# Attention without transposed probabilities: a second score product with keys on partitions, sums by paired GpSimd adds, three projection banks

## What is computed

```python
Q = (layernorm(x) @ Wq + bq)        # 16 x 224 x 512, split into 16 heads
K = (ctx @ Wk + bk)                 # 16 x 750 x 512
V = (ctx @ Wv + bv)
scores = Q K^T / sqrt(32) * gate    # gate: per key, from a second context tensor
out = softmax(scores) V
x = x + tanh(g_xattn) * (out @ Wo + bo)
x = x + tanh(g_ffn) * ffn(layernorm(x))   # shared and routed experts, top 2 of 16
```

## Time and profile before

| | |
|---|---|
| median of 3 executions | 2176.14 us |
| the profiled execution, span of its core | 2176.1 us |
| first batch's loop, from the first V product on | 69.0 to 162.3 us |
| batches 1 to 14, each | 94.7 us |
| last batch and the end of the attention | 1487.6 to 1581 us |
| experts phase | about 595 us |
| busy in the span | PE 94%, PEld 77%, DVE 58%, ACT 44%, POOL 27% |
| DMA | 307 MB, mean 141 GB/s |

### The profile page before, as it was taken

The page is one execution under the profiler, slowest core; times in us unless marked ns, Lnnn a source line. Parts: engine busy times, 40 slices in busy tenths (PEclk is TensorE's granted clock), DMA queues, the critical chain, the costliest instruction groups (busy, mean ns, idle before and its releaser), DMA issues. The chain is left out here.

```text
span 2176.1 us, 43249 instructions
## 1 busy us (share of the span) xinstructions
PE 2043.5 (94%) x13700; PEld 1677.6 (77%) x13701; DVE 1272.2 (58%) x2344; ACT 953.6 (44%) x1983; POOL 582.8 (27%) x682
## 2 busy tenths in 40 slices
PE   4999999999999999999999999999716999999999
PEld 4788888988888898888879888887514666678887
DVE  4557565665756566575666657565584333345555
ACT  0456565645656464565646556465411222210000
POOL 4222231322213132221313212130034333323331
PEclk9999999999999999999999999999956999999999
DMA  5645555554555555455555545554273444435543
GB/s 176 174 115 158 134 136 153 130 144 116 157 135 136 151 131 145 121 150 138 136 154 129 144 126 143 140 137 110 54 302 95 145 144 145 145 107 168 168 139 115
DMA packets 176438, 307.17 MB, mean 141 GB/s; under 512 B 29344, under 2 KB 86688, under 8 KB 176048
## 3 DMA queue, kind: packets, MB, share of 16 engines
q1 hardware_dynamic: 163008, 265.30, 44.4%
q0 software_dynamic: 10880, 33.56, 5.6%
q10 hardware_dynamic: 2512, 7.82, 0.9%
HBM read 145.03 MB, written 63.24 MB: 96 GB/s over the span
## 5 line engine op out<-in xcount | busy, mean ns | idle before, releaser
L631 DVE TENSOR_REDUCE neg_max<-score 112x1 f32<-112x750 f32 x512 | 455.9, 932 | 46.5 <-PE score L843 42.4
L463 ACT ACTIVATE probs<-score,neg_max 112x750 f32<-112x750 f32 x512 | 448.1, 883 | 74.1 <-DVE neg_max L631 72.7
L866 PE MATMUL flip<-ident,probs 112*125 112x112 f32 x3072 | 420.6, 274 | 9.3 <-ACT probs_t L471 8.2
L471 ACT ACTIVATE probs_t<-flip 125x448 f32<-125x448 f32 x512 | 276.6, 543 | 328.4 <-PE flip L866 328.0
L866 PEld LDWEIGHTS flip<-ident,probs 112*125 112x125 f32 x3072 | 387.4, 188 | 41.6 <-ACT probs_t L471 15.7
L361 POOL TENSOR_TENSOR k_lo<-fresh,k_hi 128x376 fp32r<-128x376 f32 (+1 forms) x128 | 118.2, 923 | 448.3 <-ACT k_hi L491 448.3
L843 PE MATMUL score<-k_stack,q_stack 128*112 128x512 f32 (+1 forms) x1024 | 232.7, 348 | 3.2 <-ACT probs L463 3.2
L815 PE MATMUL proj<-ctx_hi,wk_hi 128*128 128x376 f32 (+1 forms) x512 | 183.7, 359 | 8.3 <-POOL ctx_lo L361 6.2
L639 DVE TENSOR_SCALAR probs_t<-flip 125x448 f32<-125x448 f32 x256 | 158.1, 617 | 45.8 <-PE flip L866 45.6
L815 PE MATMUL proj<-ctx_lo,wk_hi 128*128 128x376 f32 (+1 forms) x512 | 172.0, 336 | 0.0
L815 PE MATMUL proj<-ctx_hi,wk_lo 128*128 128x376 f32 (+1 forms) x512 | 171.9, 336 | 0.0
(11 more groups left out here) (189 smaller groups left out, 3175.9 us busy)
## 6 DMA issues: line engine op xcount, KB each, us to landing
k_stack<-k_hi SPq DMA_DIRECT2D x512, 93.8 KB, 2.2
k_stack<-k_lo SPq DMA_DIRECT2D x512, 93.8 KB, 2.2
q_stack<-q_parts SPq DMA_DIRECT2D x128, 224.0 KB, 3.6
ctx_raw<-in_ctx_t SPq DMA_DIRECT2D x64, 375.0 KB, 5.3
y_slots<-y_sb SPq DMA_DIRECT2D x72, 256.0 KB, 3.1
x_in<-in_x SPq DMA_DIRECT2D x16, 448.0 KB, 5.5
q_parts<-q_hi SPq DMA_DIRECT2D x64, 112.0 KB
q_parts<-q_lo SPq DMA_DIRECT2D x64, 112.0 KB
```

The lines of the kernel that those rows point to most:

```text
L463: act.activation(probs[0:QW, h % 2, t, :], score[t][0:QW, 0:S], ACT.Exp, bias=neg_max[:, h % 2, t:t + 1], accum_out=row_sum[:, t, h:h + 1] ...
L471: act.activation(probs_t[0:KW, h % HC, 2 * p:2 * p + 2, :].rearrange("k a q -> k (a q)"), flip[(3 * h + p) % 2][0:KW, 0:2 * L], ACT.Relu). ...
L631: nc.vector.tensor_reduce(neg_max[:, h % 2, t:t + 1], score[t][0:QW, 0:S], axis=AX.X, op=ALU.max, negate=True).then_inc(maxed[t], 1)
L866: ins = nc.tensor.transpose(flip[g % 2][0:KW, k * L + t * QW:k * L + (t + 1) * QW], probs[0:QW, h % 2, t, kt * KW:(kt + 1) * KW], ident[0: ...
```

## The change

The transposes of the probabilities go, and with them `probs`, `flip_probs`, `copy_flipped`, `reciprocals` and `spread_reciprocals`.

- A second score product, `score_columns`, has keys on partitions: `k_stack` is now the stationary side (98 rows x 125 keys) and `q_stack` the moving side (224 queries). For each head there are six of them, two to a tick; a group of four heads has 12 ticks, which are worked through in three phases of four ticks (one tick per head). ACT takes the exponential of a tick from PSUM straight into `probs_t` (`exponential`), 125 x 448, without a bias.
- The maximum is brought in by the product itself. The first score product (`score_rows`) stays and serves the maximum alone, in a single buffer of two banks, six heads ahead of the attended one. `split_shift` splits the maxima of a group in two parts, `turn_shift` transposes them on PE, `copy_shift` copies them out, and `place_shift`, a DMA in ACT's list, puts them into two further rows of `q_stack`, against rows of ones in `k_stack`.
- The row sums are made from the transposed tiles. POOL adds each phase's tiles, two heads at a time, into `acc` (`add_first`, `add_pair`: 10 adds of 125 x 448 per group), and `sum_up` multiplies `acc` with a matrix of ones, which sums over partitions and spreads over 32 rows at once. `normalize_output` on DVE takes the reciprocal of 128 x 224 sums.
- `attend` is cut into three calls per group, one per phase.
- The projection has three PSUM banks (`bank_of`) with semaphores of their own in place of one; `project_out` uses them too, and its eight products, the projections and the transposes are dealt out in small pieces between the ticks.
- The stack has 96 rows (three parts): per group 12 DMAs into `k_stack` and 2 into `q_stack` in place of 16 and 2, for all 16 heads (before: 8). `k_hi`, `k_lo`, `q_hi`, `q_lo` hold two groups (before: four).
- Work changes engines: the high part of the context, the scaling of the normalization, and the copies of transposes go from DVE to ACT; two of four context remainders and the query remainders go from POOL to DVE. `store_cols` goes from ACT's to SP's queue.
- Before the loop: K before Q, V items 0 to 3 in place of item 0, and scores of heads 0 to 5 in place of head 0.

The core of the diff:

```diff
+LOWEST = -3.4028234e38
...
+BODY = ("V4", "V5", "O0", "SH1", "O1", "XT0", "XT1", "K0a", "Q0", "K0b", "SH2", "Q1", "K1a",
+        "K1b", "K2a", "K2b", "K3a", "SH3", "K3b", "YT0", "YT1", "LG", "V0", "V1", "SH0", "V2", "V3")
+OF_LAST = ("O0", "O1", "YT0", "YT1", "LG")
+SETUP = ("XT0", "XT1", "K0a", "Q0", "K0b", "Q1", "K1a", "K1b", "K2a", "K2b", "K3a", "K3b", "V0", "V1", "V2", "V3", "SH0")
...
+BEFORE = len(SETUP) + len(FIRST) - ITEMS
...
-        probs = sb("probs", [P, 2, QT, S])
-        probs_t = sb("probs_t", [P, HC, KT, L])
+        probs_t = sb("probs_t", [P, 2, HC, 2 * L])
+        acc = sb("acc", [P, HC, L])
...
-        score = [ps(f"score{t}", [P, 1024]) for t in range(QT)]
-        flip = [ps(f"flip{i}", [P, 512]) for i in range(2)]
-        proj = ps("proj", [P, 512])
...
+        score = ps("score", [P, 1024])
+        st = [ps(f"st{i}", [P, 512]) for i in range(2)]
+        proj = [ps(f"proj{i}", [P, 512]) for i in range(BANKS)]
         pv = ps("pv", [P, 512])
...
-                    for row in range(4):
-                        k_sb = k_hi if row < 2 else k_lo
-                        sp.dma_start(k_stack[row * DH:(row + 1) * DH, ring * HC + j, :].bitcast(F32),
-                                     k_sb[j * DH:(j + 1) * DH, c, :].bitcast(F32)).then_inc(k_stacked[ring], 16)
...
-                    sp.dma_start(q_stack[rep * 64:(rep + 1) * 64, ring * HC:(ring + 1) * HC, :].bitcast(F32),
-                                 q_dram[bass.ds(n, 1), c, :, :, :, :].rearrange("a j w p q -> (a w p) j q"))\
-                        .then_inc(q_stacked[ring], 16)
...
+                for rows, w in (((0, 2 * DH), (0, 2)), ((2 * DH, ROWS), (0, 1))):
+                    sp.dma_start(q_stack[rows[0]:rows[1], c * HC:(c + 1) * HC, :].bitcast(F32),
+                                 q_dram[bass.ds(n, 1), c, :, w[0]:w[1], :, :].rearrange("a j w p q -> (a w p) j q"))\
+                        .then_inc(stacked[c], 16)
+                for j in range(HC):
+                    for row, k_sb in enumerate((k_hi, k_hi, k_lo)):
+                        sp.dma_start(k_stack[row * DH:(row + 1) * DH, c * HC + j, :].bitcast(F32),
+                                     k_sb[j * DH:(j + 1) * DH, c % 2, :].bitcast(F32)).then_inc(stacked[c], 16)
...
-                nc.gpsimd.tensor_tensor(rec_x[:, :, :].rearrange("p t (h w) -> p (t h) w", w=DH),
-                                        rec[:, :, :].rearrange("p t h -> p (t h)").unsqueeze(2).broadcast_to([QW, QT * HC, DH]),
...
+            def add_first(b, c, pair):
+                if pair == 0 and not (isinstance(b, int) and b == 0 and c == 0):
+                    pool.wait_ge(summed, b * DC + c)
+                pool.wait_ge(exped, ticks(b, c, 2 * pair + 2))
+                nc.gpsimd.tensor_tensor(acc[0:KW, 2 * pair:2 * pair + 2, :], tiles(c, 0, pair, 0), tiles(c, 0, pair, 1),
+                                        ALU.add).then_inc(added, 1)
+            def add_pair(b, c, p, pair):
+                both = acc[0:KW, 2 * pair:2 * pair + 2, :]
+                pool.wait_ge(exped, ticks(b, c, p * HC + 2 * pair + 2))
+                pool.wait_ge(added, phases(b, c, p - 1) * PAIRS + pair + 1)
+                nc.gpsimd.tensor_tensor(both, both, tiles(c, p, pair, 0), ALU.add).then_inc(half_added, 1)
+                pool.wait_ge(half_added, (b * DC + c) * 2 * PAIRS + (p - 1) * PAIRS + pair + 1)
+                nc.gpsimd.tensor_tensor(both, both, tiles(c, p, pair, 1), ALU.add).then_inc(added, 1)
...
+            def exponential(b, c, u):
+                act.wait_ge(st_done, ticks(b, c, u) + 1)
+                p = u // HC
+                if not (isinstance(b, int) and ticks(b, c, u) < 2 * HC):
+                    if u % HC == 0:
+                        act.wait_ge(pv_done, phases(b, c, p) - 1)
+                    if u % 2 == 0:
+                        act.wait_ge(added, (phases(b, c, p) - 2) * PAIRS + u % HC // 2 + 1)
+                act.activation(probs_t[0:KW, (c * PHASES + p) % 2, u % HC, :], st[u % 2][0:KW, 0:2 * L], ACT.Exp)\
+                    .then_inc(exped, 1)
+            def place_shift(b, c, body):
+                act.wait_ge(proj_read[bank_of(body, f"SH{c}")], turn_of(body, f"SH{c}") + 1)
+                if not (isinstance(b, int) and b == 0):
+                    act.wait_ge(st_done, ticks(b - 1, c, TICKS))
+                act.dma_start(q_stack[ROWS:SHIFTED, c * HC:(c + 1) * HC, :].bitcast(F32).rearrange("r j q -> r (j q)"),
+                              shift_rows[:, :]).then_inc(shift_in, 16)
...
-                    act.wait_ge(maxed[t], b * H + h + 1)
-                    act.wait_ge(flipped, PRE["flipped"] + b * 3 * H + 3 * (h - 1))
-                    act.activation(probs[0:QW, h % 2, t, :], score[t][0:QW, 0:S], ACT.Exp,
...
-                        act.activation(probs_t[0:KW, h % HC, 2 * p:2 * p + 2, :].rearrange("k a q -> k (a q)"),
-                                       flip[(3 * h + p) % 2][0:KW, 0:2 * L], ACT.Relu).then_inc(copied_act, 1)
...
+            def split_shift(b, c, base):
+                dve.wait_ge(maxed, pieces(b, c * HC + HC, 0))
+                link(nc.vector.tensor_copy(shift[:, 0, :, :], neg_max[:, c % 2, :, :]), base)
+                nc.vector.tensor_tensor(shift[:, 1, :, :], neg_max[:, c % 2, :, :], shift[:, 0, :, :].bitcast(F32),
+                                        ALU.subtract).then_inc(shift_ready, 1)
...
+            def copy_shift(b, c, body):
...
+                nc.vector.tensor_copy(shift_rows[:, :], proj[bank][0:2 * HC * QT, 0:QW]).then_inc(proj_read[bank], 1)
...
+                links[0] += 1
+                nc.vector.tensor_scalar(pv[:, 0:L], pv[:, 0:L], LOWEST, None, ALU.max).then_inc(dve_chain, 1)
+                link(nc.vector.reciprocal(out_t[:, c, :], pv[:, L:2 * L]), base)
+                nc.vector.scalar_tensor_tensor(out_t[:, c, :], out_t[:, c, :], 0.0, pv[:, 0:L], ALU.max, ALU.mult)\
+                    .then_inc(normed, 1)
...
+            def score_rows(b, h, t):
+                if h % HC == 0 and t == 0:
+                    pe.wait_ge(stacked[h // HC], STACK_SET * (b + 1))
+                if not (isinstance(b, int) and pieces(b, h, t) == 0):
+                    pe.wait_ge(maxed, pieces(b, h, t))
+                at = 0
+                for w in HALF_N:
+                    ins = nc.tensor.matmul(score[0:QW, at:at + w], q_stack[0:ROWS, h, t * QW:(t + 1) * QW],
+                                           k_stack[0:ROWS, h, at:at + w], start=True, stop=True)
+                    at += w
+                ins.then_inc(scored, 1)
...
+            def turn_shift(b, c, body):
+                bank = take_proj(body, f"SH{c}")
+                pe.wait_ge(shift_ready, b * DC + c + 1)
+                nc.tensor.transpose(bank[0:2 * HC * QT, 0:QW],
+                                    shift[:, :, :, :].rearrange("q a j t -> q (a j t)").bitcast(F32),
+                                    ident[0:QW, 0:QW]).then_inc(proj_done[bank_of(body, f"SH{c}")], 1)
...
+            def score_columns(b, c, u):
+                if u == 0:
+                    pe.wait_ge(shift_in, 16 * (b * DC + c + 1))
+                if not (isinstance(b, int) and ticks(b, c, u) < 2):
+                    pe.wait_ge(exped, ticks(b, c, u) - 1)
+                h = c * HC + u % HC
...
-                        for t in range(QT):
-                            kt = 2 * p + k
-                            ins = nc.tensor.transpose(flip[g % 2][0:KW, k * L + t * QW:k * L + (t + 1) * QW],
-                                                      probs[0:QW, h % 2, t, kt * KW:(kt + 1) * KW], ident[0:QW, 0:QW])
...
+                    kt = u // HC * 2 + k
+                    ins = nc.tensor.matmul(st[u % 2][0:KW, k * L:(k + 1) * L], k_stack[0:SHIFTED, h, kt * KW:(kt + 1) * KW],
+                                           q_stack[0:SHIFTED, h, :], start=True, stop=True)
+                ins.then_inc(st_done, 1)
...
+            def sum_up(b, c):
+                pe.wait_ge(added, phases(b, c, PHASES) * PAIRS)
+                for j in range(HC):
+                    ins = nc.tensor.matmul(pv[j * DH:(j + 1) * DH, L:2 * L], ones_col[0:KW, :], acc[0:KW, j, :],
+                                           start=True, stop=True)
+                ins.then_inc(summed, 1)
```

1409 lines of the change are left out of this document (879 added, 530 removed).

## The result

The changed kernel takes 2366.0 us (median of 4 executions, 2362.0 to 2366.9), the kernel before in the same session 2177.0 (2176.1 to 2178.7): 1.086 times as long, 95% interval 1.085 to 1.088. Forecast were 2086 us and a gain of 4%; the change costs 8.6%.

A forecast was written before the change was run, and what follows sets the result against it. PE was taken as the bound: 94.7 - 8.2 + 2.3 = 88.8 us a batch. Start +10, fourteen batches -83, last batch -17 sum to -90 against 2176.1, giving 2086 us, range 2040 to 2150.

The forecast's parts named there:

- PE's work: Batch loop: 23.2 us of PE work removed and 15.0 added, net 8.2 us less per batch.
- The products of `score_columns`: PE in the loop: 96 new products a batch at 0.115 us, 11.0 us, ends 10.6 and 14.4.
- POOL's adds: POOL in the loop: 40 adds of 448 elements at 1.147 us, 45.9 us a batch.
- the reciprocals: DVE in the loop: four reciprocals of 224 elements a batch, 1.6 us each.
- at the fp32 rate: Rival: score_columns products take 0.20 us, 97 us a batch, 2217 us in total; chance 0.03.
- adds over 2 us: Rival: POOL's adds cost over 2 us; at 2.39 a batch is 110.6 us, total over 2400; chance 0.04.
- Waits added: Batch loop: new waits of PE on other engines' queues, 2.3 us a batch, bounds 0 and 7.
- a sign of being wrong: PE in the loop: waiting over 5 us a batch would show the forecast wrong.
- Before head 12: DVE's work ahead of that maximum, about 4.5 us against 3.2; within the single score buffer's 1.2 us a batch.
- stacked1: ACT's K3a part behind group 2's last tick waits for stack 1's 14 DMAs; PE waits 0.8 us a batch.
- stretch and blocking: Rival: POOL becomes the bound, its 61 us become 90, 93.5 us a batch, 2152 us in total; chance 0.14.
- the ends: Outside the fourteen middle batches: +10 us by the end of batch 0, -17 us in the last batch.

The follow-up runs named there:

- e11_all3_narrow: On e4_all3: GpSimd's adds 8 columns wide per head in place of 224, so most row sums are left out; 2086.8 us, 0.958 of before.
- e4_all3: The change with the edits of e1 and e2, plus VectorE's add_result before head 10's maximum and a context remainder behind it (three edits); 2154.6 us, 0.990 of before.
- e1: On the change: VectorE's result_factor moved behind the maximum of head 13, ScalarE's normalize of x_res moved to group 2; 2282.9 us, 1.049 of before.
- e2: On the change: ScalarE's key_high of K3a and K3b moved into group 3, GpSimd's two key_low one pair of adds later; 2269.0 us, 1.042 of before.
- e5: On the change: the edits of e1 and e2 together, without the third edit of e4_all3; 2174.6 us, 0.999 of before.
- e7_split: On e4_all3: the load of the context energies in two DMAs of 112 and 13 rows in place of one of 125; 2143.2 us, 0.985 of before.
- e8_split_norm: On e7_split: in the setup, normalization and context parts put ahead of ScalarE's and VectorE's waits for the energies; 2135.2 us, 0.981 of before.
- e13_split_only: On e8_split_norm: only split_shift of groups 2 and 3 moved behind the maxima of heads 12 and 16; 2118.5 us, 0.973 of before.
- e12_maxima_first: On e8_split_norm: maxima put ahead of VectorE's small work in four places, one context remainder moved behind copy_shift; 2156.0 us, 0.992 of before.
- e15_one_input: On e11_all3_narrow: each narrow add followed by a one-input GpSimd instruction over the other 432 columns; 2093.4 us, 0.962 of before.
- e10_stt: On e8_split_norm: the loop's SBUF-only VectorE TENSOR_TENSOR, TENSOR_SCALAR and CAST instructions written as SCALAR_TENSOR_TENSOR; 2134.1 us, 0.981 of before.

## Why the prediction was wrong

**Right.** PE's work. It was to be 86.5 us a batch; the table's rest is 86.4 to 87.2, and e11_all3_narrow, with PE busy 99.3 of 100 us, has a batch of 86.9. The products of `score_columns`, the term with the widest bounds, follow at 0.105 each (190.85 to 191.06 for two, in e4_all3) against 0.115 taken. POOL's adds are 1.15 each as taken from the earlier trace rows, the exponentials 0.54, the reciprocals 1.55 against 1.6 worked out from the earlier trace rows. The rivals at the fp32 rate and with adds over 2 us fall.

**Wrong, the waits.** "Waits added", sum 2.3, bounds 0 and 7. It is 11.9 us a batch, also over the 5 us that the prediction gives as a sign of being wrong. Three steps:

- *Before head 12*: the place was named, and DVE's list there was laid beside PE's, but "the factor of the result" was priced as DVE's own work. It waits for POOL's power, which stands behind a key remainder and a pair of adds, and two of its instructions and the second of `split_shift` take 1 us in place of 0.16. 5.28 us.
- *stacked1*, 0.8 taken: the exponentials' delay was counted, not what else stands on ACT behind the waiting K3a, the copies of the turned result with `route` behind them. 3.3 us in the mean.
- The bank of K0a, in no term: it hangs on `add_result`, which stands behind a remainder that moved to DVE. 1.9 us.

e1, e2, e5 and e4 show each of them.

**Wrong, the clock.** No term of the sum and no rival had it. The earlier trace rows show 1.00, and that was carried over to a PE with waits. It costs 7.3 us a batch, more than any single wait. Removing 8.3 us of waits gave 15.2 us a batch; step by step (by the table's idle), 2.9 gave 6.9 (the change to e2), 4.5 gave 6.8 (e2 to e5), 0.9 gave 1.5 (e5 to e4).

**Wrong, GpSimd beside VectorE.** The rival "stretch and blocking" was rated 0.14 since POOL's own subtraction has a narrow spread in the earlier trace rows. That row tells how POOL fares, not DVE. The rule of the Trainium skill (GPSIMD Engine Reference, Specifications) that is named there with the rival, contention with VectorE instructions of two SBUF inputs, is seen on VectorE: 1027 ns in place of 168 for `split_shift`'s second instruction. The price of adds and hold together is 3.9 us a batch (e4_all3 to e11_all3_narrow), near the 4.7 of the rival, though by another way: POOL's own instructions were not stretched by half.

**Wrong, the ends.** Batch 1's first score columns start at 194.4 us, 32 later than the earlier trace rows, where +10 was taken: the same products start at 190.9 in e4_all3, 183.7 in e7_split and 173.3 in e8_split_norm. So 3.5 us went with the three edits, 7 with the load of 125 rows and 10 with the order of the setup, and the 11 that are left are nearly the +10. The forecast had not looked at the load or at that order: PE's first product waits 32.4 us for x where it had waited 17.1. From the start of the last batch (1675.1) to the last logits (1775.1) it is 100.0, 6.5 over before, where -17 was taken; the trace shows waits for maxima, for `acc` (9.1) and half clock there, and the shares were not tried apart.

The account: 14 x (105.8 - 88.8) = 238 for the loop, 22 and 23.5 for the ends, -5 in the experts phase (590.0 us after 1775.1, against 595.0): 279, which is 2365.1 - 2086.

Would the change have been right without the waits? Nearly: e13_split_only, with all of the computation, better order and a better setup, is 2.7% faster than before, not 4%. The 2086.8 of e11_all3_narrow, so near the forecast, are no confirmation, for the adds are all but left out.

## What to carry to other kernels

When a change takes work off a full engine, the forecast for that work can be good to 1% and the sign still wrong. For each wait that is added, write down all that stands behind it on that engine, and who waits for that in turn; an instruction that waits for a fourth engine is priced by that engine's queue, not by its own length. Each us of TensorE's waits that was removed gave back 1.5 to 2.4 us here, through the clock; where they could not be removed, even useless work that fitted in them was better than none. Small VectorE instructions on the path of a maximum belong behind it, not ahead of it, once GpSimd adds run all the time, but only those for which no other engine waits: e13_split_only gained 17 us, e12_maxima_first, which moved more, lost 21.

## What the runs showed of the hardware

- TensorE was granted half its clock around the end of a stop and behind it, although it works without a pause then. In the 13 batches of the change all 26 stops of 2.4 to 5.3 us had a stretch of 6.8 us with them, 11 of the 13 of 1.9 us one of 3.4 us; without the longer stops (e5_both) it was 5 of 13, and stops of at most 1.05 us left the loop at 1.00 (e4_all3); 6.6 us of useless products a batch in the stops made the kernel 62 us faster.
- A VectorE instruction of 8 elements on SBUF takes 0.17 us alone and up to 1.08 while GpSimd runs an add of two SBUF tensors that started before it, and it ends with the add; beside a one-input GpSimd instruction of 0.55 us it takes 0.47 and ends with that (e15_one_input). The other way round, GpSimd's add took up to 1.83 us under a 750 wide VectorE remainder. The Trainium skill (SBUF — State Buffer, SBUF: two separate sides) calls the port pair an exclusive lock for the whole instruction; the trace agrees, and e10_stt shows that another form with two SBUF inputs does not help. Instructions that read PSUM (L792 to L794, L734) kept their times.
- One GpSimd instruction with one SBUF source takes 0.55 us for 432 columns, one with two 1.15 for 448.
- The row count of a DMA can double its time: a load of 125 rows of 12288 bytes, issued at 1.3 us, was waited for until 22.0 us, in two pieces of 112 and 13 until 11.8.
